# Route stage of an attention and fast-feedforward kernel: node scores of a batch's two token halves on two column halves of the array, leaf choice from two row halves

## The reference, cut to what matters

```python
def _fff(x, node_w, node_b, w1, b1, w2, b2):
    cur = jnp.zeros((N,), jnp.int32)
    for _ in range(DEPTH):                      # DEPTH = 4
        score = jnp.einsum('nd,nd->n', xf, node_w[cur]) + node_b[cur]
        cur = 2 * cur + 1 + (score >= 0).astype(jnp.int32)
    leaf = cur - N_NODES                        # one of 16 leaves
    ...
```

## Time and profile before

| | |
|---|---|
| Median of 3 runs | 3935.44 us (3934.48 to 3940.17) |
| Profiled execution | 3935.01 us; its span, from first to last instruction, 3933.2 us |
| TensorE matmul busy, over the span | 3720.3 us (95%) |
| VectorE busy | 3152.2 us (80%) |
| ScalarE busy | 2786.4 us (71%) |
| GpSimd busy | 1550.2 us (39%) |
| Mean granted TensorE clock | 0.981 of full speed |

### The profile page before, as it was taken

How to read it: one execution, slowest core, us unless ns; L and a number is a source line. 1 busy time by engine, 2 the same in 40 slices (tenths; PEclk the granted TensorE clock), 3 DMA queues, 4 the chain that set the end, 5 groups by cost and what they waited for, 6 DMA issues and landing times. The chain is left out here.

```text
span 3933.2 us, 63904 instructions
## 1 busy us (share of the span) xinstructions
PE 3720.3 (95%) x23714; PEld 1464.6 (37%) x23714; DVE 3152.2 (80%) x5433; ACT 2786.4 (71%) x3257; POOL 1550.2 (39%) x2057
## 2 busy tenths in 40 slices
PE   7997999999999999999999999999999879899999
PEld 5664222222222222222222222222222245588888
DVE  6776899999989999998999999899999433345454
ACT  4343888888888888887888788888888946522221
POOL 2320353263235325333532543253344357763330
PEclk9998999999999999999999999999999989899999
DMA  8775111111111111111101111110112069732220
GB/s 298 269 265 186 33 39 42 50 33 34 58 33 39 34 57 33 34 52 34 44 28 52 39 39 33 47 49 28 44 38 83 33 237 327 231 118 87 74 86 22
DMA packets 224553, 330.85 MB, mean 84 GB/s; under 512 B 29281, under 2 KB 165092, under 8 KB 219636
## 3 DMA queue, kind: packets, MB, share of 16 engines
q1 hardware_dynamic: 205812, 276.40, 21.3%
q0 software_dynamic: 18432, 50.36, 3.8%
HBM read 169.27 MB, written 156.34 MB: 83 GB/s over the span
## 5 line engine op out<-in xcount | busy, mean ns | idle before, releaser
L1734 DVE TENSOR_REDUCE first_rows<-psum 128x1 f32<-128x512 f32 x4000 | 2509.4, 684 | 173.1 <-PE psum L185 157.5
L1579 ACT ACTIVATE arena<-psum,exp_scale 128x1024 f32<-128x1024 f32 x2048 | 2159.8, 1111 | 275.8 <-PE psum L1439 269.8
L1455 PE MATMUL psum<-arena 128*32 128x512 f32 x8200 | 1107.5, 612 | 1.2 <-ACT arena L1579 0.6
L1619 POOL TENSOR_TENSOR arena<-arena 128x16 f32<-128x16 f32 x129 | 376.9, 2922 | 1504.0 <-ACT arena L1545 1504.0
L185 PE MATMUL psum<-arena 48*128 48x512 f16 x2048 | 649.6, 391 | 51.1 <-DVE first_rows L1734 22.8
L185 PE MATMUL psum<-first_rows 48*128 48x512 f16 x2048 | 622.7, 386 | 36.7 <-ACT arena L1539 7.7
L185 PEld LDWEIGHTS psum<-arena 48*128 48x128 f16 x2048 | 157.8, 93 | 865.2 <-DVE first_rows L1734 721.1
L185 PEld LDWEIGHTS psum<-first_rows 48*128 48x128 f16 x2048 | 154.9, 92 | 836.8 <-DVE first_rows L1734 715.1
L1439 PE MATMUL psum<-arena 50*128 50x512 f16 x2048 | 444.8, 382 | 11.6 <-ACT arena L1579 8.5
L1439 PE MATMUL psum<-first_rows 50*128 50x512 f16 x2048 | 447.3, 384 | 6.9 <-DMA first_rows<-arena 3.0
L1136 ACT ACTIVATE mix_arena<-psum,mix_arena 128x1024 f32<-128x1024 f32 x64 | 71.4, 1115 | 327.1 <-DVE mix_arena L1156 327.1
(11 more groups left out here) (186 smaller groups left out, 3944.0 us busy)
## 6 DMA issues: line engine op xcount, KB each, us to landing
scratch_split<-route_arena SPq DMA_DIRECT2D x64, 512.0 KB, 3.2
scratch_sorted_x<-route_arena SPq DMA_DIRECT2D x60, 512.0 KB, 4.7
scratch_sorted_y<-leaf_arena SPq DMA_DIRECT2D x60, 512.0 KB, 3.9
first_rows<-scratch_split SPq DMA_DIRECT2D x384, 64.0 KB, 2.2
arena<-scratch_split SPq DMA_DIRECT2D x384, 64.0 KB, 2.2
leaf_arena<-scratch_sorted_x SPq DMA_DIRECT2D x44, 512.0 KB, 5.8
leaf_start<-in_leafw SPq DMA_DIRECT2D x2, 5128.0 KB, 17.6
arena<-in_x SPq DMA_DIRECT2D x18, 512.0 KB, 4.9
```

The lines of the kernel that those rows point to most:

```text
L1455: last = nc.tensor.matmul(value_bank[32 * j:32 * j + 32, :], vaug[:, batch % 2, kt, 2 * pair + j % 2, :], prob[:, step % 2, j, :], start=k ...
L1579: nc.scalar.activation(prob[:, step % 2, 2 * h:2 * h + 2, :], score[:, 2 * h:2 * h + 2, :], ACT.Exp, scale=exp_scale[:, s % 2, s // 2:s // ...
L1619: nc.gpsimd.tensor_tensor(linv[:, c], total, minus_one, ALU.pow).then_inc(ochain, 1)
L1734: nc.vector.tensor_reduce(halfmax[:, odd, 2 * m + h, qt, c:c + 1], aux_bank[bank], AX.X, ALU.max).then_inc(bank_used[bank], 1)
```

## The change

`node_scores` gives each token half a column half of the array: half 0 writes partitions 0 to 63 of bank 4, half 1 partitions 64 to 127 of the same bank, with `tile_position` (0, 0) and (0, 64). The node weights are padded with zeros from 45 to 64 columns, and the loop over k is now the outer one, so that the two halves alternate. VectorE makes the bits of both halves by one instruction over 128 partitions. `bits` is now 512 wide and has half 0 in its upper 64 rows and half 1 in its lower 64, so `select` takes a tile of tokens from one row half and then one from the other, with the constant stored in both row halves; the two write banks 6 and 5. `selected` reads two banks with two instructions. The memset of `bits` is gone.

```diff
-    nodeT = ar.take(KC, NFFF * NODES)
+    nodeT = ar.take(KC, HALF)
...
-    bits = ar.take(SEQ, dt=BF16)
+    bits = ar.take(CH, dt=BF16)
...
             def node_scores(b):
                 wait_unit(pe, act_read, "turn", b, TURN_UNITS - 1)
-                for c in range(NCH):
-                    if b > 0:
-                        pe.wait_ge(bits_ready, NCH * b)
-                    for k in range(KC):
-                        last = nc.tensor.matmul(bank(4 + c)[0:NFFF * NODES, :], nodeT[:, k, :],
-                                                xnT[:, b % 2, k, c * CH:(c + 1) * CH], start=k == 0, stop=k == KC - 1)
-                    last.then_inc(node_full, 1)
+                if b > 0:
+                    pe.wait_ge(bits_ready, b)
+                for k in range(KC):
+                    for c in range(NCH):
+                        last = nc.tensor.matmul(bank(4)[HALF * c:HALF * (c + 1), :], nodeT[:, k, :],
+                                                xnT[:, b % 2, k, c * CH:(c + 1) * CH], start=k == 0, stop=k == KC - 1,
+                                                tile_position=(0, HALF * c))
+                last.then_inc(node_full, 1)
...
             def select(b):
 
-                pe.wait_ge(bits_ready, NCH * b + NCH)
+                pe.wait_ge(bits_ready, b + 1)
                 if b > 0:
                     pe.wait_ge(sel_ready, b)
-                for t in range(TT):
-                    last = nc.tensor.matmul(bank(6)[:, NLEAF * t:NLEAF * (t + 1)], bits[:, t * P:(t + 1) * P],
-                                            off_count[:, 0:NLEAF], start=True, stop=True)
+                for t in range(TT // NCH):
+                    for c in range(NCH):
+                        at = slice(HALF * c, HALF * (c + 1))
+                        last = nc.tensor.matmul(bank(6 - c)[:, NLEAF * t:NLEAF * (t + 1)], bits[at, t * P:(t + 1) * P],
+                                                off_count[at, 0:NLEAF], start=True, stop=True)
                 last.then_inc(sel_full, 1)
...
             def routed_bits(b):
-                for c in range(NCH):
-                    dve.wait_ge(node_full, NCH * b + c + 1)
-                    if b > 0:
-                        dve.wait_ge(sel_full, b)
-                    nc.vector.tensor_scalar(bits[0:NFFF * NODES, c * CH:(c + 1) * CH], bank(4 + c)[0:NFFF * NODES, :],
-                                            nodeb[0:NFFF * NODES], 0.0, ALU.add, ALU.is_ge).then_inc(bits_ready, 1)
+                dve.wait_ge(node_full, b + 1)
+                if b > 0:
+                    dve.wait_ge(sel_full, b)
+                nc.vector.tensor_scalar(bits, bank(4), nodeb, 0.0, ALU.add, ALU.is_ge).then_inc(bits_ready, 1)
 
             def selected(b):
                 dve.wait_ge(sel_full, b + 1)
-                nc.vector.tensor_scalar(sel[:, TT * b:TT * b + TT].rearrange("p t l -> p (t l)"), bank(6)[:, 0:TT * NLEAF],
-                                        0.0, None, ALU.is_equal).then_inc(sel_ready, 1)
+                for c in range(NCH):
+                    first_t = TT * b + TT // NCH * c
+                    ins = nc.vector.tensor_scalar(sel[:, first_t:first_t + TT // NCH].rearrange("p t l -> p (t l)"),
+                                                  bank(6 - c)[:, 0:TT // NCH * NLEAF], 0.0, None, ALU.is_equal)
+                ins.then_inc(sel_ready, 1)
...
-            link(nc.vector.memset(bits, 1.0))
...
-        "nodeT": chunks(np.concatenate([p["node_w"].T for p in ffn], 1)),
-        "nodeb": np.concatenate([p["node_b"] for p in ffn])[:, None],
+        "nodeT": chunks(np.concatenate([p["node_w"].T for p in ffn] + [np.zeros((DIM, HALF - NFFF * NODES), np.float32)], 1)),
+        "nodeb": np.concatenate(2 * ([p["node_b"] for p in ffn] + [np.zeros(HALF - NFFF * NODES, np.float32)]))[:, None],
...
-        "off_count": tree_constants().astype(bf16),
+        "off_count": np.concatenate(2 * [tree_constants()[0:HALF]]).astype(bf16),
```

More of the change, by code:

```diff
@@ L307, in _ @@
             nc.sync.dma_start(weightsT, w["weightsT"]).then_inc(weightsT_in, 16)
-            for dst, name in ((nodeT, "nodeT"), (nodeb[0:NFFF * NODES], "nodeb"), (off_count, "off_count"),
+            for dst, name in ((nodeT, "nodeT"), (nodeb, "nodeb"), (off_count, "off_count"),
                               (ident, "ident"), (column, "column"), (earlier, "earlier"),
```

## The result

The changed kernel took 3925.79 us (median of 7 runs, 3916.08 to 3928.98) against 3935.26 (7 runs, 3930.06 to 3940.81): 9.5 us less, a ratio of 0.9975 with a 95% interval of 0.9964 to 0.9986. The forecast was 3924.4, in a range of 3921.5 to 3930. The profiled execution took 3928.98 us, with a span of 3927.2; so it is one of the slower of its kernel, and only 6.0 us shorter than the one of before.

The account below looks back on a forecast made before the run. TensorE's instruction stream was taken to bound the route stage; node scores -12.0 us and leaf choice +1.0 us sum to -11.0 us, a forecast median of 3924.4 us, range 3921.5 to 3930.

Parts of the forecast that it names:

- The bound: Route stage: other engines follow TensorE, so a microsecond off its stream in the batches should be one off the end.
- The node scores: Node-score matmuls in each batch: the two halves run side by side, 1.85 us in place of 3.56, saving 1.71 us.
- Which batches count: Seven of the route stage's batches, not batch 0, where TensorE waits 4.19 us for GpSimd; 12.0 us saved.
- The leaf choice: Leaf matmuls from two row halves: 0.14 us more in each batch, taken at +1.0 us over seven, bounds -0.7 to +2.6.
- the 0.21 us: Price of entering and leaving the row-tiled state around the leaf choice, taken from the pair of 48-row matmuls.
- The rest at nothing: VectorE's bits and leaf instructions, the memset and 20 KB more constants: no cost; leaf instructions uncovered at most 3.8 us.
- No overlap: Rival at the node scores: the halves do not run together, leaving only the leaf choice's +1.0 us, 3936.4; 4%.
- emptying at each alternation: Rival in node scores and leaf choice: every alternation between tiles empties the array, +11.8 us, 3947.2; 3%.
- The stores: Rival in the route stage: waits for stores eat the gain in batches 1 to 3, leaving 5.8 us, 3929.6; 8%.
- the prediction's own signs of being wrong: Node rows 0.43 us apart, ScalarE waiting for a store, TensorE for GpSimd after batch 0, or a second half-clock stretch.
- The clock rival: One more half-clock stretch, behind batch 0's wait or at a stage's start, would leave -7.4 us, 3928.0; 5%.
- a microsecond or so of scatter to each side: Scatter allowed around the main case's total, with the leaf choice's bounds giving 3921.5 to 3927 us; that case 80%.

Follow-up runs that it names:

- twice: The changed kernel with the node scores of batches 0 and 4 computed twice over, same output; one run, 3926.62 us.
- serial: The changed kernel with each half's node scores on all 128 columns, zero-padded, so the halves cannot run side by side; median 3932.05 us, ratio 1.0.
- masked: The changed kernel with the leaf choice from the whole array, 4 matmuls of 128 rows and 96 columns, one VectorE instruction; median 3924.42 us, ratio 0.9976.
- early: The changed kernel with VectorE normalising 4 of the 8 tiles of batch 1; median 3926.80 us, ratio 0.9979 to the kernel before.
- again: The changed kernel unaltered, timed in a second set of runs and profiled a second time; median 3921.48 us, ratio 0.9974 to the kernel before.

## Why the prediction was right

**The bound.** TensorE's stream was the length of the route stage from batch 1 on. `twice` shows it from the other side: 1.72 us more work was 1.74 us more time, at once. The stream is not without holes: in batches 1 to 6 TensorE stands three times for VectorE, in a usual batch 0.73, 0.21 and 0.22 us. The prediction didn't price these; they are the same before and after, so the saving went through them whole.

**The node scores.** 3.56 - 1.85 = 1.71 us was forecast and 3.56 - 1.86 = 1.70 measured. The rows that carried it were those of other stages with the same form. That the two agree to 0.01 us is closer than the working deserves: the time for entering and leaving came from a group of four tiles of 32 columns. `serial` shows that the overlap is the cause: without it, and with all else changed, the kernel is as slow as before.

**Which batches count.** Seven, as forecast. Batch 0's saving went into the wait for GpSimd, which grew from 4.19 to 5.17 us and ended at the same 42.44. The reason given was right but half the story: where the scores come early, as in `masked`, TensorE is not the bound ahead of the wait either.

**The leaf choice.** The term was right in sign and too large: +0.14 us a batch forecast, +0.08 measured, 0.5 us over seven batches in place of 1.0. Both parts were a little cheaper: entering and leaving 0.09 and 0.08 us in place of 0.21 together, the four pairs 0.12 in place of 0.15. The measured gap of 0.52 us lies below the 0.55 to 0.65 that the prediction asked to see. By the rule of the Trainium skill ("TensorEngine Tiling (Array Packing)", section Instruction Overhead), eight steps of 25 ns, it was estimated at +0.19; the trace doesn't agree, since the two matmuls of a pair start 3 ns apart and the group became 0.1 us shorter. The advice there, not to split a small dimension, held all the same: this half of the change is a loss, and `masked` does the same work with less. One figure of the prediction is wrong by its own numbers: without the 0.21 us its sum would be 7 x 0.21 = 1.5 us better, not 1.

**The rest at nothing.** Right: VectorE's added 0.15 us a batch, beside a bits instruction of 0.74 us less, left TensorE's three waits for it as they were.

**The sum.** -11.0 us forecast; the batches gave 7 x 1.62 = 11.3; the medians -9.5 and, in the second set, -11.1. The mechanism carries the 11; that the median came within 1.4 us of the forecast is partly luck, with single runs 12.9 us apart. The store moved by 12.4 and, in the second profile, 9.6 us, where the forecast had 11.0: the difference goes with the clock.

**The rivals.** No overlap, and emptying at each alternation, are ruled out. The stores took back 0.3 us in batch 1 of one profile of the changed kernel, none in the other, and 0.5 us in `masked` and `twice`; with `early` they showed what they would take from a faster kernel. So two of the prediction's own signs of being wrong did appear, a wait of ScalarE for a store (0.2 us) and, in `again`, a second stretch at the half clock (3.4 us in the tail); both were small. The clock rival was given the wrong place and too little weight: it was sought behind batch 0's wait, where the first profile had less of it than before and the second as much, and not in the attention stage, where ten executions spread over 10.6 us with it. The forecast's "a microsecond or so of scatter to each side" is the number that failed: the runs of one kernel lie 9 to 15 us apart, and three sets of runs of the kernel before have medians of 3935.26, 3932.63 and 3935.46.

## What to carry to other kernels

Two independent f32 matmuls of 64 columns, 512 wide, each on its own half of the array's columns, took the time of one (1.87 us for the group in place of 3.56), in either order of writing; look for the same form elsewhere in the trace to price such a change. The row split of the 48-column matmuls did not pay for the time added around it (0.52 us in place of 0.45): putting the two constants side by side and widening the matmul was cheaper (0.40). And before taking time off the bounding engine, follow the next queue: the wait ahead of the first store cost at most 0.5 us in a batch here, and 6 us, with the fall of the clock behind it, once the stage was 4 us ahead.

## What was not expected of the hardware

An untouched stage of 2790 us changed its length by up to 10.6 us between the ten profiled executions, in step with the time that TensorE spent at 1.2 GHz in it (61 to 89 us; 0.35 us of length for each). In every profile TensorE waits at the same two places of each 348 us batch, 1.42 and 1.43 to 1.46 us, 160 waits in all. Behind 134 of them the clock falls, no later than 2.3 us after the wait; behind 26 it doesn't, and what decides is open. The changed kernel's profile shows both falls in seven batches running: what happens in one batch tends to happen in the next. And pairs of column tiles overlapped fully (1.87 us for eight rows) when both matmuls of one half were written before the other's.
